# A residual added by a product of the unit matrix, in an attention and mixture-of-experts layer on one core

## The reference, cut to what matters

```python
x = x + attention(_layernorm(x), w_q, w_k, w_v, w_o)   # x: 2 x 512 x 512, 32 heads of 16
x = x + experts(_layernorm(x), gate_w, w1, w2, w3)     # 8 experts of 800, each token goes to its best 2

out = softmax(q k^T / 4) v              # for each head
attention = out @ w_o.T
logits = xt @ gate_w.T; probs = softmax(logits); the two best, divided by their sum, are the weights
expert e: (silu(xt @ w1[e].T) * (xt @ w3[e].T)) @ w2[e].T
```

## Time and profile before

| | us |
|---|---|
| median of 3 runs | 568.57 |
| the three runs | 568.17, 568.57, 572.58 |
| the profiled execution | 568.12 |
| its span, first to last instruction | 566.3 |
| TensorE busy | 542.8 (96%) |
| VectorE busy | 390.8 (69%) |
| ScalarE busy | 323.4 (57%) |
| GpSimd busy | 127.8 (23%) |
| mean granted TensorE clock | 0.993 |

### The profile page before, as it was taken

The page is one execution under the profiler, slowest core; times in us unless marked ns, Lnnn a source line. Parts: engine busy times, 40 slices in busy tenths (PEclk is TensorE's granted clock), DMA queues, the critical chain, the costliest instruction groups (busy, mean ns, idle before and its releaser), DMA issues.

```text
span 566.3 us, 9787 instructions
## 1 busy us (share of the span) xinstructions
PE 542.8 (96%) x3520; PEld 393.4 (69%) x3520; DVE 390.8 (69%) x729; ACT 323.4 (57%) x480; POOL 127.8 (23%) x154
## 2 busy tenths in 40 slices
PE   7999999999999999999998999999999999999991
PEld 5886665333333333333677988999999999999981
DVE  6914656999999999971579987664828465566650
ACT  4322114777777777778346563747656565757540
POOL 3300111000221211451301113234340321331212
PEclk9999999999999999999999999999999999999997
DMA  8290368827557752002284499694664757486112
GB/s 325 102 111 2 51 84 90 114 40 90 74 78 94 91 74 89 21 12 87 95 316 124 148 339 341 173 331 87 236 197 136 271 148 282 93 301 167 41 30 36
DMA packets 31116, 78.19 MB, mean 138 GB/s; under 512 B 9692, under 2 KB 10972, under 8 KB 26586
## 3 DMA queue, kind: packets, MB, share of 16 engines
q1 hardware_dynamic: 25770, 68.84, 46.3%
q0 software_dynamic: 5296, 8.69, 8.1%
HBM read 53.11 MB, written 9.32 MB: 110 GB/s over the span
## 4 chain that ended last, share of the span: by engine, by line
PE 83%; DVE 10%; DMA 3%; issue 2%; POOL 1%; ACT 1%; POOLq 0%; DVEq 0%; ACTq 0%
PE ps L713 17%; PE ps L715 16%; PE ps L714 16%; PE ps_o L725 11%; PE ps L744 8%; DVE neg_max L1399 5%; PE ps_m L744 4%; PE ps L756 2%; DMA xn<-xn_rows,from_now 1%; PE ps_m L977 1%; PE ps_m L713 1%; PE ps_o L713 1%; DVE xnT_lo L1425 1%; PE ps_m L714 1%; PE ps_o L715 1%
## 5 line engine op out<-in xcount | busy, mean ns | idle before, releaser
L1183 ACT ACTIVATE probs_t<-ps 128x1024 f32<-128x1024 f32 x128 | 124.0, 1021 | 42.1 <-PE ps L756 42.1
L1399 DVE TENSOR_REDUCE neg_max<-ps 128x1 f32<-128x512 f32 x171 | 111.5, 682 | 10.5 <-PE ps L744 7.9
L713 PE MATMUL ps<-xgT_hi,w_hi 128*128 128x256 f32 (+7 forms) x384 | 110.6, 288 | 0.9 <-DVE xgT_lo L1657 0.8
L714 PE MATMUL ps<-xgT_lo,w_hi 128*128 128x256 f32 (+7 forms) x384 | 109.7, 286 | 0.0
L715 PE MATMUL ps<-xgT_hi,w_lo 128*128 128x256 f32 (+7 forms) x384 | 109.7, 286 | 0.0
L744 PE MATMUL ps<-k_stack,q_stack 48*128 48x512 f32 x171 | 73.0, 461 | 2.6 <-issue 0.3
L713 PEld LDWEIGHTS ps<-xgT_hi,w_hi 128*128 128x128 f32 x384 | 72.7, 189 | 1.4 <-DVE xgT_lo L1657 0.9
L714 PEld LDWEIGHTS ps<-xgT_lo,w_hi 128*128 128x128 f32 x384 | 72.7, 189 | 0.1
L715 PEld LDWEIGHTS ps<-xgT_hi,w_lo 128*128 128x128 f32 x384 | 72.7, 189 | 0.0
L725 PE MATMUL ps_o<-probs_t,v_ones 128*32 128x512 f32 x512 | 68.2, 605 | 0.0
L1674 DVE TENSOR_TENSOR act<-gate,ps 128x256 f32<-128x256 f32 (+7 forms) x48 | 20.7, 430 | 66.1 <-PE ps L715 52.8
(11 more groups left out here) (315 smaller groups left out, 990.7 us busy)
## 6 DMA issues: line engine op xcount, KB each, us to landing
w_sb<-w SPq DMA_DIRECT2D x16, 1024.0 KB, 7.1
w_sb<-w SPq DMA_DIRECT2D x8, 1536.0 KB
w_sb<-w SPq DMA_DIRECT2D x8, 1152.0 KB, 8.2
q_stack<-q_hi SPq DMA_DIRECT2D x32, 128.0 KB, 5.4
k_stack<-k_hi SPq DMA_DIRECT2D x32, 128.0 KB, 5.0
q_stack<-q_lo SPq DMA_DIRECT2D x16, 128.0 KB, 4.5
k_stack<-k_lo SPq DMA_DIRECT2D x16, 128.0 KB, 6.0
q_hi<-o_norm SPq DMA_DIRECT2D x16, 128.0 KB, 4.4
```

The costliest lines, as they stand in the source:

```text
L713: pe.matmul(o, x_hi, w_hi, start=start, stop=False)
L714: pe.matmul(o, x_hi, w_lo, start=False, stop=False)
L1183: a.activation(probs_t[:, kc % 2, 2 * half:2 * half + 2, :], ps4[:, 2 * (n % 2):2 * (n % 2) + 2, :], ACT.Exp, scale=D ** -0.5).then_inc(s_ ...
L1399: v.tensor_reduce(neg_max[:, g % 2, col:col + 1], max_bank(g, u2), AX.X, ALU.max, negate=True).then_inc(s_mx, 1)
```

## The change

The residual of the second batch is no longer added by VectorE. Ahead of each of these tiles' products TensorE multiplies the 128x128 unit matrix by the tile of x, in f32, into the same bank, as the first of the accumulated products (it waits for the load of x). ScalarE copies the finished bank to `x1` (`kept`), counted by a new semaphore `s_keep`; VectorE takes the statistics from the bank in PSUM, counted by `s_spread`, and scales from `x1` once it is copied. The waits on `s_res` for the second batch become waits on `s_keep`. Besides, the product `o_norm` of the last group of attention moves from GpSimd to VectorE, ahead of the statistics of tile 2.

```diff
--- before.py
+++ after.py
@@ -233,6 +233,7 @@
         s_woh, s_wol = sem("s_woh"), sem("s_wol")
         s_oh, s_ol = sem("s_oh"), sem("s_ol")
         s_endh, s_endl = sem("s_endh"), sem("s_endl")
+        s_spread, s_keep = sem("s_spread"), sem("s_keep")
         s_sum, s_part, s_partc = sem("s_sum"), sem("s_part"), sem("s_partc")
         s_const = sem("s_const")
         s_dve = sem("s_dve")
@@ -620,7 +621,7 @@
             pool.wait_ge(s_job, len(jobs))
             prepare(3)
 
-            for g in range(NG):
+            for g in range(NG - 1):
                 pool.wait_ge(s_sh, g + 1)
                 if g >= 2:
                     pool.wait_ge(s_oc[g % 2], 16 * (g // 2))
@@ -634,7 +635,7 @@
                         pool.wait_ge(s_woh, c + 1)
                         pool.tensor_tensor(wo_lo[:, c, :], wo_sb[:, c, :], wo_hi[:, c, :].bitcast(f32),
                                            ALU.subtract).then_inc(s_wol, 1)
-                if g % 2 == 1 and g < NG - 1:
+                if g % 2 == 1:
                     c = g // 2
                     for done in s_oc:
                         pool.wait_ge(done, 16 * (c + 1))
@@ -812,13 +813,16 @@
                 b, qt = divmod(t, TPB)
                 pe.wait_ge(s_wol, HC)
                 at = slice(qt * P, (qt + 1) * P)
+                if b and c0 == 0:
+                    pe.wait_ge(s_x[b], 32)
+                    pe.matmul(o, ident[:, :], x1[:, t, :], start=True, stop=False)
                 for c in range(c0, c1):
                     n = b * HC + c
                     if n < NG // 2 - 1:
                         pe.wait_ge(s_ol, n + 1)
                     else:
                         pe.wait_ge(s_endl, 1)
-                    last = three(o, o_hi[:, n, at], o_lo[:, n, at], wo_hi[:, c, :], wo_lo[:, c, :], c == 0, c == HC - 1)
+                    last = three(o, o_hi[:, n, at], o_lo[:, n, at], wo_hi[:, c, :], wo_lo[:, c, :], b == c == 0, c == HC - 1)
                 if c1 == HC:
                     last.then_inc(s_op, 1)
 
@@ -871,7 +875,7 @@
 
                 pe.wait_ge(s_gw, 16)
                 pe.wait_ge(s_t2e, t1)
-                pe.wait_ge(s_res, TPB + n + 1)
+                pe.wait_ge(s_keep, n + 1)
                 o = ps4[:, n, 0:(t1 - t0) * P].rearrange("p (t n) -> p t n", t=t1 - t0)
                 for c in range(HC):
                     last = pe.matmul(o[32 * c:32 * c + 32, :, :], gw_pad[:, c, :], xn2T[:, t0:t1, c, :],
@@ -883,7 +887,7 @@
                 pe.wait_ge(s_sum, 1)
                 pe.wait_ge(s_or, NG)
                 if n == 1:
-                    pe.wait_ge(s_res, TPB + 3)
+                    pe.wait_ge(s_keep, 3)
                 pe.wait_ge(s_partc, n + 1)
                 for t in range(t0, t1):
                     last = pe.matmul(lg_banks[n][:, t * E:(t + 1) * E], lg_t[:, n, (t - t0) * P:(t - t0 + 1) * P],
@@ -893,7 +897,7 @@
             def logits(t):
 
                 pe.wait_ge(s_t2e, t + 1)
-                pe.wait_ge(s_res, NT)
+                pe.wait_ge(s_keep, TPB)
                 for c in range(HC):
                     last = pe.matmul(lg_banks[2][:, t * E:(t + 1) * E], xn2T[:, t, c, :], gw_pad[:, c, 0:E],
                                      start=(c == 0), stop=(c == HC - 1))
@@ -1183,6 +1187,11 @@
                         a.activation(probs_t[:, kc % 2, 2 * half:2 * half + 2, :], ps4[:, 2 * (n % 2):2 * (n % 2) + 2, :],
                                      ACT.Exp, scale=D ** -0.5).then_inc(s_ex, 1)
 
+            def kept(t):
+
+                a.wait_ge(s_spread, t - TPB + 1)
+                a.activation(x1[:, t, :], ps4[:, t % TPB, :], ACT.Copy).then_inc(s_keep, 1)
+
             def turned(t):
 
                 a.wait_ge(s_t2, t + 1)
@@ -1215,14 +1224,18 @@
             a.activation(o_hi[:, NG // 2 - 1, :], o_all[:, NG // 2 - 1, :], ACT.Copy).then_inc(s_endh, 1)
             for t in range(3):
                 turned(t)
+            kept(4)
             root(B + 5, 4, 5)
+            kept(5)
             root(B + 6, 5, 6)
             turned(3)
             split13(0, 0)
+            kept(6)
             root(B + 7, 6, 7)
             turned(4)
             turned(5)
             parts_out(0, TPB)
+            kept(7)
             root(B + 8, 7, 8)
             turned(6)
             parts_out(1, TPB - 1)
@@ -1436,8 +1449,7 @@
 
                 v.wait_ge(s_x[t // TPB], 32)
                 v.wait_ge(s_op, t + 1)
-                o = max_bank(t, "projection") if t < TPB else ps4[:, t % TPB, :]
-                v.tensor_tensor(x1[:, t, :], o, x1[:, t, :], ALU.add).then_inc(s_res, 1)
+                v.tensor_tensor(x1[:, t, :], max_bank(t, "projection"), x1[:, t, :], ALU.add).then_inc(s_res, 1)
 
 
             def spread_x1(t0, t1):
@@ -1473,6 +1485,10 @@
                             v.wait_ge(s_on, g)
                         v.stream_shuffle(rec_all[:, :], rec_row[:, :], [1] * 32).then_inc(s_sh, 1)
 
+            v.wait_ge(s_sh, NG)
+            v.wait_ge(s_oc[(NG - 1) % 2], 16 * (NG // 2 - 1))
+            v.tensor_tensor(o_norm[:, (NG - 1) % 2, :], o_raw[:, (NG - 1) % 2, :], rec_all[:, :],
+                            ALU.mult).then_inc(s_on, 1)
             spread_x1(2, 3)
             residual(3)
             scaled(xn2, x1, 2, 3, s_xn2)
@@ -1482,10 +1498,14 @@
                             ALU.subtract).then_inc(s_endl, 1)
             scaled(xn2, x1, 3, 4, s_xn2)
             for t in range(TPB, NT):
-                residual(t)
+                v.wait_ge(s_op, t + 1)
+                v.bn_stats(stats[:, t, :], ps4[:, t % TPB, :]).then_inc(s_spread, 1)
+                v.wait_ge(s_spread, t - TPB + 1)
+                variance(t, t + 1)
                 if t > TPB:
+                    v.wait_ge(s_keep, t - TPB)
                     scaled(xn2, x1, t - 1, t, s_xn2)
-                spread_x1(t, t + 1)
+            v.wait_ge(s_keep, TPB)
             scaled(xn2, x1, NT - 1, NT, s_xn2)
 
             v.wait_ge(s_const, N_CONST)
```

## The result

| | before | after |
|---|---|---|
| median, us | 568.96 (20 runs) | 571.62 (20 runs) |
| profiled execution, us | 568.12 | 571.3 |
| its span, us | 566.3 | 569.6 |

The ratio of after to before is 1.0051, with a 95% interval of 1.0034 to 1.0067: slower by some 3 us, and the interval leaves out no change. The forecast was 571.2, with 569.0 to 573.5. Two of the 20 runs after, 687.1 us at a mean granted clock of 0.703 and 1005.65 us, stand far from the others and are not in the ratio.

A forecast was written before the change was run, and what follows sets the result against it. TensorE carried 83% of the chain, VectorE pacing tiles 6 and 7. Normalisation 0.0 plus 3.0 us from unit products and ScalarE's queue, on 568.12, gave 571.1 to 571.6, stated as 571.2; range 569.0 to 573.5.

The forecast's parts named there:

- The price of a unit product: TensorE's f32 unit-matrix product ahead of each second-batch tile: 0.86 us each, 3.44 for four.
- the formula: Shift of the kernel's time for p us per unit product: 4p - 0.26 - 0.17; 0.5 at p = 0.227, 4.4 at 1.21.
- Tile 3's transposes: On TensorE behind the second batch's projection: start moves from 291.80 to 294.98, 3.18 us later.
- Router products: TensorE's router products of tiles 4 to 6, waiting for ScalarE's tile 6 copy: from 297.45 to 300.46.
- the walk through ScalarE's queue: From tile 3's copy at 295.61 through split, keeps, roots and copies to tile 6's copy at 299.78, 3.01 us later.
- The hole before the last chunk: TensorE's 0.26 us wait before 286.93 for the last group's low half; closes as unit products make TensorE later.
- part 1: Last group's normalisation moved from GpSimd to VectorE: worth 0.0, ends -0.26 and +0.2; o_hi at 285.47 instead of 285.43.
- Case (a): Rival: VectorE's relief decides if a unit product costs below 0.11 us; 567.9, at best 567.7; chance 0.05.
- Case (b): Rival: TensorE's products alone count, ScalarE's copies of tiles 6 and 7 not queueing; 2.3 later, 570.4; chance 0.12.
- Case (d): Rival: the delay is absorbed in later gathers or first-expert splits; between 568.3 and 570; chance 0.12.
- case (c): Rival: more delay, from products at 1.21 us (572.5) or a clock fall around 299 to 300 (576 or so); chance 0.14.
- the fill and a VectorE scaling can lie side by side at their usual length: GpSimd's w2_sb fill, moved to about 277.8 beside VectorE's scaling; up to 0.53 us lost by the skill, sum unchanged.

The follow-up runs named there:

- e4: The changed kernel with each unit product issued twice, the first result overwritten; ratio to the kernel before 1.0097, clean time 574.77 us against 568.56.
- e3: The changed kernel with ScalarE's list reordered, keeps 6 and 7 and their roots ahead of transposed copies; ratio to before 1.0028, clean time 570.27 us against 568.56.
- e1: The kernel before with only the last group's normalisation moved from GpSimd to VectorE; ratio to before 0.9994, clean time 568.54 us against 568.56.
- e2: The changed kernel with the last group's normalisation back on GpSimd; ratio to before 1.0045, clean time 570.93 us against 568.56.
- e5: The changed kernel without the four unit products, x left out of the second batch's sum, so later stages do other work; time 612 us.
- run 40: Not a follow-up run: "run" is a verb here, for 40 fillers of TensorE, 4.53 us in the trace before and 5.05 after.
- e6: The changed kernel with x added by two f32r products, high part from ScalarE, low from GpSimd; ratio to before 1.0054, clean time 571.21 us against 568.92.
- e7: The changed kernel with the f32r pair, low parts from GpSimd, and ScalarE's list reordered; ratio to before 1.0031, clean time 570.91 us against 568.92.
- e10: The kernel before with a unit product for tile 6 alone, without eight fillers, ScalarE's list reordered; ratio to before 0.999, clean time 568.77 us against 569.31.
- e11: The kernel before without the two groups of four fillers around the router products of tiles 0 to 3; ratio 0.9989, clean time 568.69 us against 569.31.
- e8: The changed kernel with the f32r pair, low parts from VectorE, last normalisation on GpSimd; ratio to before 1.0018, clean time 570.07 us against 569.31.
- e9: The changed kernel with f32r pair, low parts from VectorE, normalisation on GpSimd, ScalarE's list reordered; ratio to before 1.0019, clean time 569.76 us against 569.31.
- e12: The kernel before with tile 6's unit product alone, no eight fillers, weight split behind tile 7's root; ratio to before 1.0, clean time 568.72 us against 569.06.

## Why the prediction was right

- The sum was right in size: 3.0 us forecast from the profiled execution; the median moved by 2.66 (2.5 without the two far runs), the clean times of the experiments' before and of after differ by about 2.5, and B by 2.82. All three are a little less than the forecast. The forecast of 571.2 stands 0.4 below the median after.
- The price of a unit product was the largest unknown, between 0.227 and 1.21. I took 0.86 from the two instructions of the router's f32 product less their tails; it is 0.86 in e4 and in the chain; four times the f32r product, 0.91, would have been too much. Doubling the products moved B by 3.54, where the formula gives 3.44.
- Tile 3's transposes: 294.98 forecast, 295.02 in the trace. Keep 6: 297.06 and 297.10. Keep 7: 299.17 and 299.10. Tile 6's copy: 299.78 and 299.67. Router products: 300.46 and 300.40. That these agree within 0.1 is partly luck, for the passage began 0.13 later after than before. Counted from its start, A moved by 3.09 (3.18 forecast) and B by 2.82 (3.01 forecast). The hole was worth more than its 0.26: the first product behind a wait also takes 0.31 instead of 0.23 to the next start (286.93 to 287.24 before), 0.35 in all, and 3.44 - 0.35 is 3.09. From A to B the gain was 0.27 and not 0.17. e3 shows that the walk through ScalarE's queue was more than a matching list of times: with the queue reordered, 0.71 us goes.
- The hole before the last chunk was filled as forecast, and part 1 was worth nothing in time: o_hi started at 285.88, which is 0.4 later than forecast, but the shuffle was 0.38 late itself; e1 and e2 show the zero from both sides. In e1 the hole itself had moved to the transposes of tile 2, which neither the prediction nor the expectation had.
- Case (a) needed a product below 0.11 and fell with its price, 0.86; e5 bears out its other half, that ScalarE's queue then gives some 0.2 and no more. Case (b) fell with e3: TensorE alone makes 2.11 and not 2.82. Case (d), absorption, did not happen: the gather stands 3.25 us later, the span is 3.3 longer. Of case (c), the clock did fall between 305 and 309, on top of the forecast. The shift is 2.95 at the router products, 3.01 at the first gather (305.30 and 308.31), 3.26 at the first expert products (311.68 and 314.94) and 3.25 at the late gather. Over the first part of that stretch run 40 fillers of TensorE, before and after:

```profile
304.59 4.53 PE L762 MATMUL ps<-idle_b 128*128 128x256 bf16 x40
```

```profile
307.60 5.05 PE L763 MATMUL ps<-idle_b 128*128 128x256 bf16 x40
```

They took 0.52 longer in the stretch of the fallen clock, and TensorE, which had waited 0.21 for the gathered rows at 310.26, no longer waited for them. So that the clock made the last 0.25 is likely; no run shows it by itself.
- One sentence was wrong: that the fill and a VectorE scaling can lie side by side at their usual length. In the trace before they shared only 0.14 us (283.02 to 283.16), which I had not worked out. After, a scaling of 0.55 took 0.88. It cost nothing, because VectorE waited 1.01 us for the shuffle behind it, and that half of the sentence was right.
- One step is missing from the sum: after tile 7's root VectorE waited 0.23 between the reciprocal and the scaling, so that xn2 was written to 300.86 and not 300.66, 3.2 later than before; the chain runs there.

## What to carry to other kernels

Work moved from the engine that paces a stage to one that is ahead costs at once all that exceeds what the second is ahead by: here TensorE had a hole of 0.26 us at the place and was given 3.44. What the first engine saves comes back only where it had set the pace, 0.98 here, and only if nothing else stands in between. Follow the other engines' queues for that, instruction by instruction: copies that look free by the share of busy time stood behind one that waits for the very engine that was made late, and took 0.71 of it. If x must be added by products, a high and a low part in f32r cost half of one f32 product (0.46 against 0.86), provided that the parts are made where they lengthen nothing: made by GpSimd they lengthened VectorE's normalisation by 0.41 and 0.67 (e6, e7).

## What the runs showed of the hardware

**VectorE beside GpSimd.** The two scalings of tiles 0 and 1 take 1.00 us together in the trace before (two of 0.55, overlapping). In the changed kernel they took 1.33 (0.53 and 0.88), in e1 1.49. The fill of w2_sb has moved beside them; GpSimd's timeline after, and that of e3, where the same two scalings (277.99, 1.00 together) kept their length:

```profile
278.12 0.53 POOL L647 MEMSET w_sb<- 128x512 f32 x1
```

```profile
277.63 0.53 POOL L647 MEMSET w_sb<- 128x512 f32 x1
```

In e3 the fill was nearly over when the scalings began (it ended at 278.16, and they shared 0.17). In the changed kernel it reached 278.65, into the second one, which began at 278.49 and was lengthened by 0.33; in e1 it reached 278.78, and the second one, from 278.47, took 1.04. The Trainium skill (SBUF — State Buffer, "Who interferes with whom") says that GpSimd and a VectorE instruction in a two-port mode share a port pair, which the one that issues first holds for its whole length while the other stands. The first scaling, begun at 278.04 and so ahead of the fill, kept its usual time, and the second was lengthened: both agree. That the fill shows its usual 0.53 beside the first scaling, and that the shared 0.17 of e3 lengthened nothing, does not. The same section has a VectorE instruction with two inputs in SBUF contend with a GpSimd instruction that reads SBUF: the normalisation of e6, 1.10 instead of 0.69 beside a GpSimd subtraction, and 1.36 in e7, agree.

**The granted clock.** In the changed kernel it fell to half between 305 and 309, where it had been full in the trace before (these are TensorE's two levels, 2.4 and 1.2 GHz):

```profile
305.00:306.00 1.00, 0.92 (x19) 0.80 (x20) 0.77 (x7) 1.00 (x2) 0.00 (x0) 0.64 0.00 0
306.00:307.00 1.00, 1.00 (x7) 0.68 (x5) 1.00 (x2) 1.00 (x2) 0.00 (x0) 0.50 0.00 0
...
308.00:309.00 1.00, 1.00 (x8) 0.78 (x7) 0.86 (x6) 0.99 (x2) 0.69 (x1) 0.65 0.00 0
309.00:310.00 1.00, 1.00 (x12) 0.90 (x10) 0.86 (x6) 0.03 (x1) 0.70 (x2) 1.00 0.00 0
```

TensorE had been busy for 7.74 of the 8.00 us to 300 and for 4.65 of the 5.00 to 305 before it fell. In e1 the same fall came at 301 to 305, in e10 and e11 at 299 to 307, in e3 and e4 not at all up to 316, and it follows neither part of the change: e1 and e2, each without one of them, both have it. Over a whole kernel the times go with the mean clock: of the changed kernel's runs, those at 0.992 and 0.993 took 570.7 to 571.1, those at 0.987 took 572.2 to 572.5, those at 0.980 and 0.981 575.3 to 576.6. The kernel before shows the same spread in its 35 runs beside e8 to e11 (568.7 at 0.992, 575.6 at 0.975), so it is no effect of the change; but it is larger than the effect, and medians over few runs must be read with it. What sets these falls off stays open.

**Small transfers.** The shuffle of the last group, which waits for a transfer of 8 KB, came 1.2 (e2, e3) to 1.9 us (e5) after the start of tile 4's projection in different executions of kernels that are alike up to there, and 1.97 in e6. Where TensorE waits for the last chunk or for the scaling of tile 2, which hang on it, this goes into A and B: e1, e5, e6, e9 and e12 show it.
